# Recurrent gated attention and feed-forward on one core: level 1 by elementwise products, levels 32 and 64 in column groups, state outputs by row groups, gelu into PSUM, and all stages in a new order

## The reference

```python
def _gla_scan(q, k, v, g):
    S0 = jnp.zeros((q.shape[-1], v.shape[-1]), q.dtype)
    def step(S, inp):
        qt, kt, vt, gt = inp
        S = jnp.exp(gt)[:, None] * S + kt[:, None] * vt[None, :]
        return (S, qt @ S)
    return jax.lax.scan(step, S0, (q, k, v, g))[1]
...
o = o * jax.lax.rsqrt(jnp.mean(o * o, axis=-1, keepdims=True) + EPS) * rms_w
o = o.reshape(b, t, DV) * jax.nn.silu(x @ Wg)
return o @ Wo
...
x = x + _layernorm(_L0_attn_ref(_layernorm(x, axis=-1), ...), axis=-1)
x = x + _layernorm(_L0_ffn_ref(_layernorm(x, axis=-1), ...), axis=-1)
```

## Time and profile before

| | before |
|---|---|
| median of 3 runs | 1316.63 us (1313.33 to 1316.76) |
| the profiled execution's own time | 1313.97 us |
| its span | 1312.2 us |
| PE busy | 94% |
| DVE busy | 80% |
| ACT busy | 54% |
| POOL busy | 48% |
| granted TensorE clock, mean | 0.988 |

### The profile page before, as it was taken

How to read it: one execution, slowest core, us unless ns; L and a number is a source line. 1 busy time by engine, 2 the same in 40 slices (tenths; PEclk the granted TensorE clock), 3 DMA queues, 4 the chain that set the end, 5 groups by cost and what they waited for, 6 DMA issues and landing times. The chain is left out here.

```text
span 1312.2 us, 23418 instructions
## 1 busy us (share of the span) xinstructions
PE 1230.2 (94%) x8372; PEld 1073.7 (82%) x8372; DVE 1044.8 (80%) x2404; ACT 711.3 (54%) x1443; POOL 635.0 (48%) x893
## 2 busy tenths in 40 slices
PE   5889999999999999999999999999999999999957
PEld 3677889888897888889888788988889888897956
DVE  3769788796978979787787978879697896978863
ACT  5365555656456465644756555565545646465423
POOL 5436353563445544564435635356354554456431
PEclk9989999999999999999999999999999999999988
DMA  3110010100101001010011001010010100100000
GB/s 97 38 33 17 17 49 1 54 17 17 49 21 49 1 17 49 21 49 1 17 49 53 16 17 49 1 54 16 17 49 21 48 2 17 49 21 33 1 17 17
DMA packets 31778, 38.27 MB, mean 29 GB/s; under 512 B 2448, under 2 KB 29104, under 8 KB 31664
## 3 DMA queue, kind: packets, MB, share of 16 engines
q1 hardware_dynamic: 31136, 36.25, 8.3%
q10 hardware_dynamic: 528, 0.52, 0.1%
HBM read 28.38 MB, written 8.39 MB: 28 GB/s over the span
## 5 line engine op out<-in xcount | busy, mean ns | idle before, releaser
L1047 POOL TENSOR_TENSOR k_decayed<-k_decayed,block_totals 128x256 f32<-128x256 f32 x192 | 168.2, 876 | 277.1 <-PE ps_level L298 276.6
L298 PEld LDWEIGHTS ps_level<-q_blockdiag,k_decayed 128*128 128x128 f32 x1792 | 227.1, 191 | 51.5 <-DVE q_blockdiag L585 41.1
L298 PE MATMUL ps_level<-q_blockdiag,k_decayed 128*128 128x128 f32 x1792 | 241.1, 278 | 26.4 <-DVE q_blockdiag L585 25.1
L575 DVE COPY_PREDICATED attn_T<-level_masks,ps_level 128x512 f32<-128x512 uint32 x160 | 152.7, 954 | 16.0 <-PE ps_level L298 16.0
L585 DVE TENSOR_TENSOR q_blockdiag<-q_blockdiag,block_totals 128x512 f32<-128x512 f32 x192 | 141.3, 736 | 28.1 <-PE ps_level L298 28.1
L1053 POOL TENSOR_TENSOR rstd<-rstd,minus_half 128x1 f32<-128x1 f32 x192 | 111.7, 584 | 106.6 <-DVE rstd L636 106.6
L255 PE MATMUL ps_big<-w_ff_hi,h_hi 128*128 128x256 f32 x512 | 150.1, 293 | 3.0 <-DVE h_lo L590 3.0
L257 PE MATMUL ps_big<-w_ff_hi,h_lo 128*128 128x256 f32 x512 | 144.8, 283 | 0.0
L256 PE MATMUL ps_big<-w_ff_lo,h_hi 128*128 128x256 f32 x512 | 144.7, 283 | 0.0
L837 ACT ACTIVATE gelu_out<-ps_big,ff_b_cols 128x512 f32<-128x512 f32 x128 | 88.0, 688 | 79.8 <-PE ps_big L257 43.2
L623 DVE SCALAR_TENSOR_TENSOR o<-o,o_rstd,out_gate 128x128 f32<-128x128 f32 x256 | 93.3, 426 | 45.0 <-POOL o_rstd L1068 45.0
(11 more groups left out here) (113 smaller groups left out, 3155.1 us busy)
## 6 DMA issues: line engine op xcount, KB each, us to landing
w_raw<-L_ffn_w SPq DMA_DIRECT2D x16, 1024.0 KB, 5.6
out<-y SPq DMA_DIRECT2D x16, 512.0 KB, 2.9
x_in<-L_attn_x SPq DMA_DIRECT2D x15, 512.0 KB, 3.9
ff_b_rows<-L_ffn_b SPq DMA_DIRECT2D x8, 128.0 KB, 2.6
x_in<-L_attn_x ACTq DMA_DIRECT2D x1, 512.0 KB, 4.0
w_raw<-L_attn_Wv SPq DMA_DIRECT2D x1, 512.0 KB, 6.0
w_raw<-L_attn_Wg SPq DMA_DIRECT2D x1, 512.0 KB, 7.1
y<-L_attn_Wo SPq DMA_DIRECT2D x1, 512.0 KB, 8.1
```

The lines of the kernel that those rows point to most:

```text
L298: last = nc.tensor.matmul(PL[tl][:, c * CH:(c + 1) * CH], kk[:, tl, c * CH:(c + 1) * CH], q[:, :, :, 1, :], start=True, stop=True)
L575: nc.vector.copy_predicated(dst, m.to_broadcast([P, 2 * NCH, HC // h, h]), src)\
L1047: nc.gpsimd.tensor_tensor(k, k, t.to_broadcast([P, n, h]), ALU.mult)\
```

## The change

- Level 0 (h = 1) leaves PE, `q_update` and `k_update`. POOL multiplies the even keys by the decay (`pair_keys`), DVE multiplies these with the odd queries straight from the projection (three products of 256 elements in `q_evac` where one of 512 was), `diag_rows` sums them with 8 more matmuls of 64 columns, a second transposition and a second small copy follow, and one COPY_PREDICATED of 1024 elements (`copy_level0`) puts them into `attn_T`. ACT writes the decayed keys back (`k_pairs`).
- Levels 5 and 6 (h = 32 and 64) multiply only the blocks that are needed, each in a column group of the array: 8 matmuls of 32 by 64, or 4 of 64 by 128, a half level. `copy_blocks` takes 4 copies of 128 elements, or 2 of 256, where it took 2 of 256, or 1 of 512.
- The products of queries and state take 64 partitions each (row groups) and go with the rest of `att` to two banks, `ps_out` and `ps_state`.
- gelu writes to the transposes' PSUM banks, and `f2` writes to the second halves of the level banks.
- Each engine's stages are in a new order: a level's halves together, then two `f1`; `gp(2)`, `vp(3)`, `gp(3)` of a sequence between its first levels; `f2` spread over the first half of the chunks; the last layer norm of the scan behind the next level 1.

The diff, cut to its core:

```diff
         o = sb("o", [P, 2, DV])
         ogT_hi, ogT_lo = sb("ogT_hi", [P, VT, CH], F32R), sb("ogT_lo", [P, VT, CH], F32R)
-        hf = sb("gelu_out", [P, 2, T])
+        hf = sb("gate_and_q", [P, 2, T])
         gm = qg = hf
+        m1 = xh[:, 2:4, :].rearrange("p a d -> p (a d)").rearrange("p (k n) -> p k n", k=KT)
+        p1 = o[:, 0, :].rearrange("p (k n) -> p k n", k=KT)
         h_hi, h_lo = sb("h_hi", [P, FT, T], F32R), sb("h_lo", [P, FT, T], F32R)
         NA = 3 * D
...
-                    if i == 0:
-                        if tl == 0:
-                            pe.wait_ge(sem["ac_qb"], at("ac_qb", s, 2 * KT))
...
-                            if C:
-                                pe.wait_ge(sem["dv_o"], at("dv_o", p, NCH * H))
-                            pe.wait_ge(sem["ac_k"], at("ac_k", s, KT))
+                    if i == 1:
+                        pe.wait_ge(sem["ac_qb"], at("ac_qb", s, 2 * (tl + 1)))
+                        pe.wait_ge(sem["ac_k0"], at("ac_k0", s, 1))
                         if C:
-                            pe.wait_ge(sem["dv_t"], at("dv_t", p, 3 + tl))
+                            pe.wait_ge(sem["dv_t"], at("dv_t", p, tl + 1))
                     else:
-                        pe.wait_ge(sem["dv_qu"], at("dv_qu", s, 2 * (i - 1) + tl + 1))
-                        pe.wait_ge(sem["po_ku"], at("po_ku", s, 2 * (i - 1) + tl + 1))
+                        pe.wait_ge(sem["dv_qu"], at("dv_qu", s, lv(i - 1, tl)))
+                        pe.wait_ge(sem["po_ku"], at("po_ku", s, lv(i - 1, tl)))
                         if i - 1 < MASKED:
-                            pe.wait_ge(sem["dv_cp"], at("dv_cp", s, 2 * (i - 1) + tl + 1))
+                            pe.wait_ge(sem["dv_cp"], at("dv_cp", s, lv(i - 1, tl)))
                         else:
-                            pe.wait_ge(sem["ac_cp"], at("ac_cp", s, 2 * tl + 2))
+                            pe.wait_ge(sem["ac_cp"], at("ac_cp", s, 6 * tl + 4))
                     for c in range(NCH):
-                        q = qbd[:, tl, :, c * CH:(c + 1) * CH].rearrange("p a (n t h) -> p a n t h", t=2, h=h)
-                        last = nc.tensor.matmul(PL[tl][:, c * CH:(c + 1) * CH],
-                                                kk[:, tl, c * CH:(c + 1) * CH], q[:, :, :, 1, :],
-                                                start=True, stop=True)
+                        if i < MASKED:
+                            q = qbd[:, tl, :, c * CH:(c + 1) * CH].rearrange("p a (n t h) -> p a n t h", t=2, h=h)
+                            last = nc.tensor.matmul(PL[tl][:, c * CH:(c + 1) * CH],
+                                                    kk[:, tl, c * CH:(c + 1) * CH], q[:, :, :, 1, :],
...
+                    if C:
+                        pe.wait_ge(sem["dv_t"], at("dv_t", p, 3))
                     for tl in range(KT):
                         for c in range(NCH):
-                            last = nc.tensor.matmul(PO[32 * c:32 * (c + 1), 0:CH], ind[:, tl, :],
-                                                    qk[:, tl, c * CH:(c + 1) * CH], start=(tl == 0), stop=(tl == KT - 1))
+                            r = slice(32 * c, 32 * (c + 1))
+                            nc.tensor.matmul(PO[r, 0:CH], ind[:, tl, :], qk[:, tl, c * CH:(c + 1) * CH],
+                                             start=(tl == 0), stop=(tl == KT - 1))
+                    for tl in range(KT):
+                        for c in range(NCH):
+                            r = slice(32 * c, 32 * (c + 1))
+                            last = nc.tensor.matmul(PO[r, CH:CH + HC], ind[:, tl, :], p1[:, tl, c * HC:(c + 1) * HC],
+                                                    start=(tl == 0), stop=(tl == KT - 1))
                     last.then_inc(sem["pe_drow"], 1)
...
                         pe.wait_ge(sem["dv_xlo"], at("dv_xlo", s, kt + 1))
                     transpose_tokens(xh, kt).then_inc(sem["pe_xt"], 1)
@@ -381,7 +405,7 @@
                         pe.wait_ge(c_lo, 1)
                     pe.wait_ge(sem["dv_xlo"], at("dv_xlo", n, KT))
                     if C:
-                        pe.wait_ge(sem["dv_y4"], at("dv_y4", p, 3 + tl))
...
+                    for tl in range(KT):
+                        w = slice(tl * HV, (tl + 1) * HV)
+                        for hh in range(2):
+                            hd = 2 * tl + hh
+                            last = nc.tensor.matmul((PO, PS)[hh][:, w], Am[:, tl, 2 * c + hh, :],
+                                                    v[:, c, hd * HV:(hd + 1) * HV], start=True, stop=(c == 0))
+                        for hh in range(2 if c else 0):
+                            r = slice(hh * HK, (hh + 1) * HK)
+                            last = nc.tensor.matmul((PO, PS)[hh][:, w], qbd[r, tl, hh, c * CH:(c + 1) * CH],
+                                                    S[r, tl, :], start=False, stop=True)
...
+                def levels(i):
+                    level(i, 0)
+                    level(i, 1)
+
+                if B:
+                    levels(1)
+                    gp(2, s)
+                    vp(3, s)
+                    diag_rows()
+                    levels(2)
+                    gp(3, s)
+                    diag_columns()
+                if C:
+                    x3t(0)
+                    x3t(1)
...
+                        f1(2 * (i - 3))
+                        f1(2 * (i - 3) + 1)
+                if C:
...
+                def copy_level0():
+
+                    dve.wait_ge(sem["dv_dg"], at("dv_dg", s, 2))
+                    dve.wait_ge(sem["dv_cp"], at("dv_cp", s, lv(3, 1)))
+                    n = KT * NCH * 2
+                    dst = Am[:, :, :, :].rearrange("p k a (n t) -> p (k a) n t", t=2)[:, :, :, 1]
+                    m = masks[:, 0, :].bitcast(U32).rearrange("p (a n) -> p a n", a=1)
+                    src = h1[:, :].rearrange("p (a n) -> p a n", n=1)
+                    nc.vector.copy_predicated(dst, m.to_broadcast([P, n, HC]), src.to_broadcast([P, n, HC]))\
+                        .then_inc(sem["dv_c0"], 1)
...
-                    nc.vector.tensor_tensor(h_lo[:, m, :], hf[:, m % 2, :], h_hi[:, m, :].bitcast(F32),
+                    nc.vector.tensor_tensor(h_lo[:, m, :], PT[m % 2][:, :], h_hi[:, m, :].bitcast(F32),
                                             ALU.subtract).then_inc(sem["dv_hlo"], 1)
...
+                    dve.wait_ge(sem["po_m1"], at("po_m1", n, 1))
+                    dve.wait_ge(sem["po_tot"], at("po_tot", n, 1))
+                    if B:
+                        dve.wait_ge(sem["pe_ogt"], at("pe_ogt", s, 3))
+                    q = PB[tl][:, :].rearrange("p (n t) -> p n t", t=2)
+                    nc.vector.tensor_tensor(p1[:, tl, :], q[:, :, 1], m1[:, tl, :], ALU.mult).then_inc(sem["dv_q"], 1)
+                    d = qg[:, tl, :].rearrange("p (n t) -> p n t", t=2)
+                    a = ga[:, tl, :].rearrange("p (n t) -> p n t", t=2)
+                    nc.vector.scalar_tensor_tensor(d[:, :, 0], q[:, :, 0], QSCALE, a[:, :, 0],
                                                    ALU.mult, ALU.mult).then_inc(sem["dv_q"], 1)
-
+                    nc.vector.scalar_tensor_tensor(d[:, :, 1], q[:, :, 1], QSCALE, totals(2)[:, tl, :],
+                                                   ALU.mult, ALU.mult).then_inc(sem["dv_q"], 1)
+
...
+                if B:
+                    copy_pairs(2, 0)
+                    q_update(2, 1)
+                    copy_pairs(2, 1)
+                    pair_columns()
+                if C:
+                    x3_lo(0)
+                    x3_lo(1)
+                if B:
+                    q_update(3, 0)
+                    copy_pairs(3, 0)
+                    q_update(3, 1)
+                    copy_pairs(3, 1)
+                    copy_level0()
+                if C:
+                    h_lo_part(0)
+                if B:
+                    q_update(4, 0)
+                    copy_pairs(4, 0)
+                    q_update(4, 1)
+                    copy_pairs(4, 1)
+                if C:
+                    h_lo_part(1)
+                    h_lo_part(2)
+                if B:
+                    q_update(5, 0)
+                    q_update(5, 1)
...
+                    nc.scalar.activation(PT[m % 2][:, :], PB[m % 2][:, :], ACT.Gelu_apprx_tanh,
                                          bias=b1s[:, m:m + 1]).then_inc(sem["ac_gelu"], 1)
                     act.wait_ge(sem["ac_gelu"], at("ac_gelu", p, m + 1))
-                    copy(h_hi[:, m, :], hf[:, m % 2, :], "ac_hhi")
+                    copy(h_hi[:, m, :], PT[m % 2][:, :], "ac_hhi")
...
+                    act.wait_ge(sem["pe_lv"], at("pe_lv", s, lv(i, tl)))
                     for b in range(HC // h):
-                        r = slice(2 * h * b, 2 * h * b + h)
-                        copy(Am[r, tl, :, 2 * h * b + h:2 * h * (b + 1)],
```

(20 more changed lines are left out.)

501 lines of the change are left out of this document (273 added, 228 removed).

## The result

The changed kernel takes 1351.53 us (median of 4 runs, 1351.44 to 1351.89) beside 1316.37 us for the kernel before on the same chip: a ratio of 1.0267, 95% interval 1.0255 to 1.028. It is slower by 35 us. The forecast was 1304 us, and its range ended at 1332.

What follows compares the result with a forecast made beforehand. PE was taken to bound the kernel, DVE to set its waits. Terms -1.6 - 1.2 - 0.25 + 0.45 + 2.0 gave -0.6 us a round, -10 us for 16: 1304 us, range 1262 to 1332.

Steps and rivals of the forecast that it cites:

- The wait of level 6: Level 6's second half waits for ten ACT copies though eight free its bank: 3.5 us of PE wait, 1.5 its own.
- the term of -0.25: State outputs in row groups: -1.35 us a round from side-by-side passes, +1.1 for changes of array division; -0.25 taken.
- the slower bound: State outputs' upper bound of +1.1 us a round: nothing runs side by side and array changes are paid.
- row groups do not run side by side: Rival, chance 0.14: 24 state passes keep 0.11 us each, changes cost 1.1 on top; +0.75 us a round, 1326 us.
- Weight splits, bias and x loads move along with slack: Claim that this work fits in spare time, ACT being busy 44 of 78 us; no cost in the sum.
- the term of -1.2: PE's levels 5 and 6 in column groups: -1.2 us a round, bounds -0.9 and -1.5.
- gelu into PSUM: ACT's gelu left at 0.69 us, bounds -0.1 and +0.1 each, 8 a round; low part from PSUM taken as 0.6.
- The copy of 1024: DVE's level 0 copy of 1024 elements: 2.5 us, twice the 1.3 of 512; bound 1.25.
- the rival of a shorter chain through ACT: Rival, chance 0.26: copy of 1024 1.25 us faster, level 6 waits 2 us, state outputs give 1.2; 1264 us.
- Level 2's waits for `q_blockdiag`: PE's waits in level 2, 2.4 us a round in the kernel before, were to go.
- `wo(3)` waits: End of a round: PE has 11.1 us of work, DVE needs 12.4 for `og_lo(3)`; wait of 1.4 us.
- DVE's end of a round: Rival, chance 0.14: norms beside POOL's work add 1.3 us a round in front of `wo(3)`; 1325 us.

Runs made afterwards that it cites:

- x4_busy: Changed kernel with its long wait kept and 7 extra useless identity products put between the halves of level 6: 1335.68 us, ratio 1.0148 to the kernel before.
- x2_full: Changed kernel with the state outputs of att(1) to att(3) over all 128 partitions again, in the same two banks: 1342.36 us, ratio 1.02 to the kernel before.
- x3_both: Changed kernel with level 6's second half waiting for 8 copies instead of 10 and state outputs over all 128 partitions: 1297.24 us, ratio 0.9856 to the kernel before.
- x1_wait: Changed kernel with level 6's second half waiting for 8 of ScalarE's copies instead of 10: 1310.20 us, ratio 0.9953 to the kernel before.
- x5_nolo: x3_both with most of POOL's low parts of w2 left out for every expert but the first: 1276.72 us, ratio 0.9709 to the kernel before.
- x8_cols: x3_both with levels 5 and 6 as full products again and ScalarE's copies in 3 pieces per half instead of 6: 1290.46 us, ratio 0.9813 to the kernel before.
- x6_oglo: x3_both with the last transposed output's high and low parts moved ahead on ScalarE and VectorE: 1295.71 us, ratio 0.9852 to the kernel before.
- x12_gelu: x8_cols with gelu written to SBUF again and its high and low parts made from there: 1316.57 us, ratio 1.001 to the kernel before.

## Why the prediction was wrong, step by step

**The wait of level 6: right in size, wrong in what comes with it.** The forecast had "3.5 us of PE wait, with `f1(6)` queued behind it"; the plain round has 3.53, the w2 round 2.0 behind a stretch at the lower clock that fills the rest. It counted "1.5 us of the 3.5 as this wait's own"; undoing it gave 41 us, 2.6 a round. The missed part is the granted clock behind the wait, a term that the sum put at nothing. The working had every duration at the full clock, and no step asked what TensorE's clock does behind a stall of that length. The kernel before gave little warning: its stretches have 0.98 and 1.00. x4_busy puts the clock in the plain round at 1.3 to 1.6 us, and at 16 us in all. The lower clock ahead of level 6 in the w2 rounds costs nothing measurable.

**State outputs, the term of -0.25: the slower bound was the truth.** "If two row groups run side by side they take half" failed in its second half: they do start together, but the pairs stand 0.21 us apart, so nothing is saved, while "0.09 a change" was right and most of the +1.1 was paid (0.32 us in each of three `att`). Both edits of x2_full and x3_both show it, the cleaner by x3_both against x1_wait: 13 us, 0.8 a round. This is the rival "row groups do not run side by side", which had 0.14, and its reason in the earlier trace rows, that loads of 128 columns follow one another every 0.11 us, fits: each pass here has a load of its own with 128 columns, and four passes take 0.43 to 0.45 us either way. That the loads are the cause is argued, not shown: the second pair's loads start 0.11 us behind the first pair's, its passes 0.21. The rule of the Trainium skill that was cited for it then ("TensorE: Matmul & The Clock Gate", section "LDWEIGHTS (loading the stationary operand)"), that a load takes by its columns and not its rows, agrees: 184 ns for 64 rows against 188 to 192 for 128. The same page of the Trainium skill, Part 3, lets loads of different row groups overlap, and that is there too: the two loads of a pair start within 0.01 us of each other.

**"Weight splits, bias and x loads move along with slack": wrong for POOL.** The paper schedule laid out one kind of round. In the w2 round POOL's pieces stand beside `q_update` at levels 3 to 5, where the new order has both halves of a level together with nothing of PE's between them. x5_nolo has them at 2.7 us in each such round, 20 us in all. In the kernel before, the two kinds of round differ by 0.55 us only the earlier trace rows. The changed kernel hides the cost: its two kinds differ by 1.1 us, because the lower clock adds 1.6 to the plain one only.

**Levels 5 and 6, the term of -1.2: wrong sign.** The passes did get shorter as worked out (level 5 0.69 us, level 6 1.19). But with the short wait x8_cols is faster without them by 7 us. The step that failed is the one that took PE's work off the round while the same edit doubled the number of ACT's copies in front of the gelus. The forecast saw those copies, and charged them to the wait for ten alone.

**gelu into PSUM, "ACT's 0.69 I leave as it is (bounds -0.1 and +0.1 each": mis-sized in what it is worth.** Gelu and the high part moved by 0.03 us, inside the bounds. The low part takes 0.69 us instead of the 0.6 that the schedule had, but with gelu back in SBUF the kernel is 26 us slower: the largest gain of any part of the change that was undone here, of which PE's waits for low parts show 15. The sum had no term for it.

**What held.** The copy of 1024 takes 2.48 us (2.5 forecast), with which the rival of a shorter chain through ACT fell. Level 2's waits for `q_blockdiag` are gone. `wo(3)` waits 1.3 us (1.4). Level 5's second half waits 0.55 (0.4). DVE's end of a round did not become the bound; x6_oglo shows a chain there that a reordering doesn't shorten.

**The sum.** The miss is 47.5 us. The clock behind the stall (16, by x4_busy), the row groups (17: 0.8 instead of -0.25 in 16 rounds) and POOL's pieces (20) make 53. The pieces cost the kernel before something too, 0.4 to 0.55 us in a w2 round, some 4 us, so about 49 of them are new. This is not a closed account: the three sizes were taken from different kernels, levels 5 and 6 are left out of it (in x8_cols they are some 26 us worse than the forecast's -19), and so is gelu's 26 the other way. Level 0's own gain was not separated: no run undid that part alone, since the order of all stages hangs on it. The kernel with the two faulty edits mended, 1297 us, is close to the 1304 forecast by luck: it carries the pieces' 20 us, which the forecast had not, and it is without the long wait, for which the forecast had 3.5 us a round.

## What to carry to other kernels

A wait written as a count over several tiles is worth checking on paper for the number that really frees the bank: here one constant cost 41 us and turned a small gain into a loss. Price a stall on TensorE of some microseconds with the work behind it too, at the lower clock, and look whether that work is followed by another wait, which would hide it. Make the schedule for every kind of round, and put operations of VectorE with two SBUF inputs where GpSimd is idle, or give them a PSUM operand; and before shortening passes on a busy engine, count what the shorter form adds in front of the engine that it waits for.

## What the runs showed of the hardware that was not expected

- Passes of float32 on two row groups with 128 columns each way: 6 or 7 ns apart within a pair, 0.21 us from pair to pair, against 0.11 us for one pass over all rows (x3_both): no gain in time.
- Behind 3.5 us in which TensorE stood still, its granted clock is at 1.2 GHz for some 3 us; with 1.8 us of those 3.5 filled by products of no use it stays at 2.4 GHz, and the whole kernel is 16 us faster for doing more (x4_busy).
- A stretch at 1.2 GHz in front of a wait that another engine ends costs nothing: w2 rounds of x4_busy take 80.7 us with it and without it (in x1_wait, where that wait is short, it costs 0.35 us). Behind that wait it costs 1.6 us: 81.4 against 79.8 in x2_full.
- A VectorE product of 128x512 with both operands in SBUF takes 0.68 us alone and up to 1.78 beside one of GpSimd, ending 0.55 us after it; with an operand in PSUM it takes 0.69. Over the whole kernel gelu's result in PSUM, which gives the low part that operand, is worth 26 us (x12_gelu).
- VectorE's masked copy takes the other engine's time as well: POOL's two updates beside it took 2.94 us instead of 1.35.
